# Three rearrangements of a four-layer kernel: the routing weights' transpose inside the pick, the last layer's loads inside its normalisation, and the third layer's indirect transfers divided differently over its stages

## The chip, the core and the metric

The kernel is one program on one core of one Trainium2 chip. The metric is the device time of one execution in microseconds. The core has five engines with a queue of instructions each: TensorE (PE), VectorE (DVE), ScalarE (ACT), GpSimd (POOL) and SyncE (SP, which here only issues transfers). GpSimd also issues the indirect transfers, the ones whose rows are chosen by an index tile.

## The reference

The input x is (8, 512, 128). Four layers follow, each of the form

```python
xn = layernorm(x)
s = attention_like(xn)      # another block in each layer
g = silu(ffn_like(xn))      # another mixture of experts or gated net in each
x = x + s * g
```

What matters here of the layers, which are numbered 0 to 3:

- Layer 1's attention keeps the outputs of only 153 of the queries of each head: a score for each query is made, and the highest 153 are picked. Its feed-forward net routes every token to 8 of 64 small experts, with weights that are normalised and scaled by 2.5.
- Layer 2's attention is a gated linear recurrence with a causal convolution of 4 taps ahead of it and unit-length keys and queries. Its feed-forward net is a mixture of 8 experts with 2 of them for each token and a capacity of 640 tokens for each expert, so tokens are packed by expert, computed, and fetched back.
- Layer 3 is softmax attention with 16 heads and a position bias, an output product and its bias `bo`, and a gated net whose weights are int32 and are scaled by 1/127.

## The kernel before, in words

Everything is resident in SBUF: `R.x` (the stream), `R.xnT` (the normalised stream, transposed), `R.s` and `R.f` (the two branches), each 128 partitions by 4096 floats. The work is a chain of phases. Each phase is one block: every engine gets its own list of instructions, waits go over semaphores, and at the end of the block all engines meet. When a phase with semaphores ends, one more short block clears them (`phase`, line 42 on). So phases never overlap; an engine that has nothing to do in a phase stands still until the slowest has finished. Eight groups of 512 tokens (B = 8, T = 512) are the usual loop inside a phase.

**Layer 1, between its attention and its output product.** `layer1_attention` runs the attention (`att1`), then `spread_phase` (line 1483), then `pick_phase` (line 1317), then the output product. `spread_phase` transposes the routing weights `comb` (32 tiles on PE, copied out of PSUM by ACT in 8 pieces) and has SP write them to DRAM as `cT` in 9 transfers, for which the block waits. VectorE meanwhile sets 4 rows of ones (`wt[NE:]`, line 1504) and clears `R.f` (line 1505). `pick_phase` is almost all VectorE: 20 rounds of `max` and `match_replace` over 128x512 scores, one after the other, with one transpose ahead of them and one behind. What it reads has nothing to do with `comb`.

**Layer 2.** `conv_phase` (16 steps c) makes queries, keys and values: PE does one product and a product of four taps a step, ACT and DVE the convolution of the values, DVE a transpose (line 2252), and POOL copies it to its place (line 2269). `unit_phase` scales queries and keys to unit length: ACT squares, PE sums, ACT and DVE take the inverse root, and then 16 products with `back` on PE (line 2318) are multiplied in by DVE (line 2330); PE may be four products ahead. Beside this work POOL issues 64 indirect scatters of 128 rows each (line 3207) that pack the tokens for the experts: two ahead of each of the 16 copies in `conv_phase`, and the other 32 one behind the other in `unit_phase`. `packed_experts_phase` waits for all of them. After `chunks_phase`, `recur_phase` runs the recurrence over 16 chunks as 8 bodies of 4 parts; POOL prepares `recur_st` for each part (line 2617) and issues an indirect gather of expert results (line 3231) behind three of the four parts, 24 in all. `output2_phase` gates and projects the result; in it POOL issues the other 40 gathers one behind the other. Its ACT and DVE combine the gathered rows in four parts (lines 2835 and 2883), each part once its own 16 gathers have landed.

**Layer 3.** `norm_phase` has an argument `ahead` for transfers that SP issues during it; for layer 3 it is empty. `layer3_attention` starts with SP issuing `bo` and eight pieces of `wo`, then the first weights, tokens and bias (lines 1827 to 1842). DVE copies `bo` into all of `R.s` (line 2043). `layer3_gate` starts with SP loading the int32 weights `wi` (line 1683), which DVE scales (line 1734) before PE can begin.

Of the kernel before, what the change touches and what calls it, by code (L numbers as in the profile page):

```python
# [8 lines left out]
P = 128  # L9
D = 128  # L10
B, T = 8, 512
NT = B * T // P
QT = T // P
# [1303 lines left out]
def pick_phase(nc, R, name, negmax, total, count, mask):  # L1317
# [3 lines left out]
    with phase(nc, name) as p:  # L1321
# [8 lines left out]
        s_sp, s_t, s_mk, s_m = p.sem("sp"), p.sem("t"), p.sem("mk"), p.sem("m")  # L1330
        scale = DH ** -0.5
        with nc.Block() as block:
            @block.vector
# [27 lines left out]
            def _(pe):  # L1361
# [3 lines left out]
                ins.then_inc(s_t, 1)  # L1365
                pe.wait_ge(s_mk, 1)
# [5 lines left out]
def layer1_attention(nc, R, t, early, out, sc, consts, s_in, comb, cT):  # L1372
    with ExitStack() as ctx:
# [12 lines left out]
        spread_phase(nc, R, "spread", comb, 64, cT)  # L1386
        pick_phase(nc, R, "pick", negmax, total, int(0.6 * 256), mask)
# [93 lines left out]


def spread_phase(nc, R, name, comb, NE, cT):

    ROWS = cT.shape[0]
    with phase(nc, name) as p:
        st = p.sb("st", [P, 2, QT, NE])
        wt = p.sb("wt", [ROWS, B * T])
        pt = p.ps("pt", [P, 2, T])
        s_one, s_st, s_t, s_wt, s_out = p.sem("one"), p.sem("st"), p.sem("t"), p.sem("wt"), p.sem("out")  # L1490
        NBODY = B // 2
        with nc.Block() as block:
            @block.sync
            def _(sp):
                sp.wait_ge(s_one, 1)
                sp.dma_start(cT[NE:, :], wt[NE:, :]).then_inc(s_out, 16)
                for n in range(B):
                    sp.wait_ge(s_wt, n + 1)
                    sp.dma_start(cT[:NE, n * T:(n + 1) * T], wt[:NE, n * T:(n + 1) * T]).then_inc(s_out, 16)
                sp.wait_ge(s_out, 16 * (B + 1))  # L1500

            @block.vector
            def _(dve):
                nc.vector.memset(wt[NE:, :], 1.0).then_inc(s_one, 1)
                nc.vector.memset(R.f[:, :, :], 0.0)

            @block.tensor
            def _(pe):
                for n in range(B):
                    if n >= 2:  # L1510
                        pe.wait_ge(s_wt, n - 1)
                    for q in range(QT):
                        ins = nc.tensor.transpose(pt[:NE, n % 2, q * P:(q + 1) * P], comb[:, n * QT + q], R.ident[:, :])
                    ins.then_inc(s_t, 1)

            @block.scalar
            def _(act):
                for n in range(B):
                    act.wait_ge(s_t, n + 1)
                    nc.scalar.activation(wt[:NE, n * T:(n + 1) * T], pt[:NE, n % 2], ACT.Copy).then_inc(s_wt, 1)  # L1520
# [145 lines left out]
def layer3_gate(nc, R, t):  # L1666

    U = 3
    with phase(nc, "glu") as p:
        wi = p.sb("wi", [P, 3, U, P], I32)  # L1670
# [6 lines left out]
        s_in, s_w, s_up, s_g, s_h, s_d, s_o, s_f = (p.sem(k) for k in ("in", "w", "up", "g", "h", "d", "o", "f"))  # L1677
        NBODY = B // 2
        IT = 2 * U
        with nc.Block() as block:  # L1680
            @block.sync
            def _(sp):
                sp.dma_start(wi[:, :, :, :].rearrange("p k u f -> p (k u f)"), t["w3"]).then_inc(s_in, 16)

# [77 lines left out]
def layer3_attention(nc, R, t):  # L1762
# [13 lines left out]
    with phase(nc, "att3") as p:  # L1776
        bias = p.sb("bias", [P, 2, 2 * BW])
        w = p.sb("w", [P, 2, 3, P])
        wo = p.sb("wo", [P, PAIRS, P])
# [11 lines left out]
        bo = p.sb("bo", [P, QT * D])  # L1791
# [4 lines left out]
        s_c = p.sem("c")  # L1796
# [27 lines left out]
        with nc.Block() as block:  # L1824
            @block.sync
            def _(sp):
                sp.dma_start(bo[:, :], t["bo3"]).then_inc(s_c, 16)
                for a in range(PAIRS):
                    sp.dma_start(wo[:, a], t["wo3"][a]).then_inc(s_c, 16)
# [1731 lines left out]
```

## Time and profile before

| | |
|---|---|
| median of 3 runs | 4108.3 us (4107.21 to 4111.95) |
| the profiled execution | 4112.44 us, of which 4110.6 us are the span from its first to its last instruction |
| PE busy | 3561.5 us (87%) |
| DVE busy | 2452.7 us (60%) |
| ACT busy | 2020.7 us (49%) |
| POOL busy | 1263.6 us (31%) |
| granted TensorE clock, mean | 0.911 of full speed |

The page's second part cuts the span into 40 slices of some 103 us; the busy tenths of PE, the granted clock and the DMA share are

```profile
PE   5799999959996788894999986788985599999997
PEclk9799999979997799996999987787687799999998
DMA  4322222100001311110666631030005233333330
```

The stages of this case lie where PE is low: slice 19 (spread and pick), slices 25 and 26 (convolution, unit length, experts), slices 30 and 31 (recurrence, output of layer 2, normalisation of layer 3), and the first and last slices of layer 3.

### The profile page before, as it was taken

The numbers are of one execution on the slowest core, as the hardware profiler recorded it, in microseconds if no ns is written. First come the engines' busy times: TensorE is split into PE (matmuls) and PEld (weight loads), VectorE is DVE, ScalarE is ACT, GpSimd is POOL, SyncE is SP. The second block draws the span as 40 slices with busy tenths as digits, with TensorE's granted clock in tenths as the row PEclk, the third lists the DMA queues.
The fourth block names the chain that finished last, engine by engine and source line by source line (L and its number), as shares of the span: only waits on it lengthen the run. The fifth ranks groups of instructions, "written<-read, shape, count | busy, mean of one in ns | idle before, by whom it ended". The sixth has DMA issues, their size and how long they took to land. (4 is left out here: it accounts for less than half of the span.)

```text
span 4110.6 us, 86910 instructions
## 1 busy us (share of the span) xinstructions
PE 3561.5 (87%) x28212; PEld 2164.2 (53%) x28212; DVE 2452.7 (60%) x5699; ACT 2020.7 (49%) x3970; POOL 1263.6 (31%) x1810
## 2 busy tenths in 40 slices
PE   5799999959996788894999986788985599999997
PEld 2344444437773222222677753268973366666664
DVE  5667677631113688885677776427645566666664
ACT  6466666633335477772333334233243465656562
POOL 0111111100001011110677762506474244444440
PEclk9799999979997799996999987787687799999998
DMA  4322222100001311110666631030005233333330
GB/s 128 79 55 57 54 58 54 48 11 6 11 6 49 76 46 43 42 30 13 176 163 157 157 83 61 34 101 3 3 17 72 80 116 114 117 113 117 114 104 27
DMA packets 198051, 287.18 MB, mean 70 GB/s; under 512 B 40922, under 2 KB 155296, under 8 KB 197460
## 3 DMA queue, kind: packets, MB, share of 16 engines
q1 hardware_dynamic: 193688, 275.28, 24.1%
q0 software_dynamic: 4096, 8.40, 1.5%
q8 instruction: 160, 2.62, 0.3%
q14 instruction: 107, 0.88, 0.1%
HBM read 232.38 MB, written 35.84 MB: 65 GB/s over the span
## 5 line engine op out<-in xcount | busy, mean ns | idle before, releaser
L709 ACT ACTIVATE att_E<-att_pX,att_gs 128x512 f32<-128x512 f32 (+3 forms) x1024 | 723.5, 740 | 423.5 <-PE att_pX L643 177.0
L742 DVE TENSOR_REDUCE att_mx<-att_pS 128x1 f32<-128x512 f32 (+4 forms) x960 | 732.4, 787 | 204.9 <-PE att_pS L617 173.0
L1855 POOL TENSOR_TENSOR att_E<-att_E,att_rz 128x128 f32<-128x128 f32 (+3 forms) x512 | 358.1, 720 | 435.3 <-DVE att_rz L2063 435.3
L637 PE MATMUL att_pX<-arr_qs,arr_ks 75*128 75x512 bf16 (+4 forms) x1536 | 427.3, 334 | 28.0 <-ACT att_E L709 12.8
L612 PE MATMUL att_pS<-arr_ks,arr_qs 72*128 72x512 bf16 (+4 forms) x1536 | 410.5, 339 | 44.1 <-DVE att_pO L732 12.6
L1583 POOL TENSOR_TENSOR pairs_h<-pairs_m,pairs_r 128x512 f32<-128x512 f32 x272 | 346.2, 1273 | 245.8 <-DVE pairs_m L1646 127.2
L574 POOL CAST att_mp<-att_m 16x128 bf16<-16x128 f32 x288 | 81.2, 282 | 935.2 <-DVE att_m L753 910.0
L1607 PEld LDWEIGHTS pairs_po<-pairs_a,pairs_h 128*128 128x128 f32 x2176 | 286.1, 192 | 130.2 <-issue 128.4
L654 PE MATMUL att_pO<-att_E,att_vs 128*9 128x512 f32 (+3 forms) x3072 | 328.9, 500 | 1.3 <-ACT att_E L709 1.3
L1628 ACT ACTIVATE pairs_r<-pairs_ph 128x512 f32<-128x512 f32 x272 | 162.6, 598 | 326.9 <-PE pairs_ph L1599 326.9
L1994 ACT ACTIVATE att_E<-att_S,att_nm 128x128 f32<-128x128 f32 (+3 forms) x512 | 282.0, 556 | 38.4 <-DVE att_nm L2057 38.4
L1599 PE MATMUL pairs_ph<-xnT,pairs_a 128*128 128x512 f32 x544 | 280.9, 599 | 10.2 <-DMA pairs_a<-in_down_dram 10.2
L637 PEld LDWEIGHTS att_pX<-arr_qs,arr_ks 79*128 79x128 bf16 (+1 forms) x1536 | 134.9, 98 | 294.1 <-ACT att_E L709 196.1
L1607 PE MATMUL pairs_po<-pairs_a,pairs_h 128*128 128x128 f32 x2176 | 287.5, 275 | 0.5 <-POOL pairs_h L1583 0.5
L1646 DVE SCALAR_TENSOR_TENSOR pairs_m<-pairs_ph,pairs_c 128x512 f32<-128x512 f32 x272 | 188.0, 692 | 140.0 <-ACT pairs_r L1628 132.8
L2057 DVE CUSTOM_DVE_ANT_0 att_S<-att_pS,att_bias 128x128 f32<-128x128 f32 (+3 forms) x512 | 230.5, 487 | 64.1 <-PE att_pS L1897 60.9
L612 PEld LDWEIGHTS att_pS<-arr_ks,arr_qs 76*128 76x128 bf16 (+1 forms) x1536 | 131.1, 99 | 240.3 <-DVE att_mx L742 149.1
L1252 PEld LDWEIGHTS ex_po<-ex_a,ex_h 128*128 128x128 f32 x1536 | 202.4, 192 | 92.0 <-issue 91.2
L1278 ACT ACTIVATE ex_h<-ex_ph,ex_bs 128x512 f32<-128x512 f32 x192 | 131.9, 687 | 214.5 <-PE ex_ph L1243 214.5
L1294 DVE SCALAR_TENSOR_TENSOR f<-ex_po,ex_ws,f 128x128 f32<-128x128 f32 x192 | 54.0, 344 | 277.4 <-PE ex_po L1252 277.4
L2071 DVE COPY att_WT<-att_pT 128x128 f32<-128x128 f32 (+2 forms) x384 | 179.2, 507 | 66.6 <-PE att_pT L1907 59.1
L1252 PE MATMUL ex_po<-ex_a,ex_h 128*128 128x128 f32 x1536 | 203.1, 275 | 0.0
(411 smaller groups left out, 6527.9 us busy)
## 6 DMA issues: line engine op xcount, KB each, us to landing
pairs_c<-weights SPq DMA_DIRECT2D x272, 256.0 KB, 3.9
att_bias<-in_bias_dram SPq DMA_DIRECT2D x64, 896.0 KB, 4.5
parts<-proj_part SPq DMA_DIRECT2D x144, 128.0 KB, 2.3
att_xb<-xnT SPq DMA_DIRECT2D x64, 256.0 KB, 2.7
arr_qs<-parts SPq DMA_DIRECT2D x192, 64.0 KB
arr_ks<-parts SPq DMA_DIRECT2D x192, 64.0 KB
att_w<-in_w3a_dram SPq DMA_DIRECT2D x64, 192.0 KB, 2.4
arr_qs<-parts SPq DMA_DIRECT2D x96, 96.0 KB
```

What stands on the lines that cost most here:

```text
L612: ins = nc.tensor.matmul(pS[:, bank, n * w:(n + 1) * w], qs[:K1, u, x, q * P:(q + 1) * P], ks[:K1, u, x, :w], start=(n == 0 or not causal) ...
L637: ins = nc.tensor.matmul(dst[:, n], ks[:, g % NB, x, kt * P:(kt + 1) * P], qs[:, g % NB, x, q0(kt):], start=(apart or n == 0), stop=not ca ...
L654: ins = nc.tensor.matmul(pO[32 * x:32 * x + DV, q0(kt):], vs[:, g % 2, x // maps, kt], E[:, kt % 2, x, :w], start=(kt == 0), stop=(kt == Q ...
L709: nc.scalar.activation(E[:, kt % 2, WIDE * xp:WIDE * (xp + 1), :w], places(c)[0], ACT.Exp, scale=gs[:, g % 2, gain_of:gain_of + 1]).then_i ...
L742: V.reduce_max(dst, src, AX.X).then_inc(s_mx, 1)
L1252: ins = nc.tensor.matmul(po[:, g % 2, q * P:(q + 1) * P], h[:, u % 2, q * P:(q + 1) * P], a2[:, v, u], start=(u == 0 and q == 0), stop=(u ...
L1583: nc.gpsimd.tensor_tensor(h[:, g % RING], m[:, g % RING], r[:, g % RING], ALU.mult).then_inc(s_h, 1)
L1599: nc.tensor.matmul(ph[:, g % RING], a[:, v, 0], R.xnT[:, b * T:(b + 1) * T], start=True, stop=True).then_inc(s_up, 1)
L1607: ins = nc.tensor.matmul(po[:, g % RING, q * P:(q + 1) * P], h[:, g % RING, q * P:(q + 1) * P], a[:, v, 1], start=True, stop=True)
L1855: nc.gpsimd.tensor_tensor(E[:, k, :width(j)], E[:, k, :width(j)], rz[:, u, k:k + 1].broadcast_to([P, width(j)]), ALU.mult).then_inc(s_n, 1)
L1994: nc.scalar.activation(E[:, k, :width(j)], S[:, r % RING, :width(j)], ACT.Exp, bias=nm[:, u, k:k + 1], scale=-1.0, accum_out=Z[:, u, k:k + ...
L2057: nc.vector.tensor_tensor_reduce(out=S[:, r % RING, :w_], in0=pS[:, r // 2 % 2, h, :w_], in1=bias[:, u, off:off + w_], scale=-1.0 / DW, sc ...
```

## The change

1. `spread_phase` is gone. Its work is inside `pick_phase`: PE does the 32 transposes of `comb` behind the first transpose of the scores, ACT copies them, SP writes them out, and the two memsets are on POOL in place of DVE. A phase with one semaphore is laid around the pick, so one more clearing block follows it.
2. In layer 3 `bo`, `wo` and `wi` have tiles in a new phase `pre3` around the whole layer, and SP loads them during `norm3`. The tiles and loads inside the two later phases are gone. One more clearing block ends the layer.
3. In `conv_phase` POOL issues three scatters ahead of each copy, in place of two; 16 are left for `unit_phase`. In `recur_phase` a gather follows every part, 32 in all; 32 are left for `output2_phase`.

```diff
 def pick_phase(nc, R, name, negmax, total, count, mask, comb, NE, cT, s_out):
+        wt = p.sb("wt", [cT.shape[0], B * T])
+        pW = p.ps("pW", [P, 2, T])
+            @block.gpsimd
+            def _(pool):
+                nc.gpsimd.memset(wt[NE:, :], 1.0).then_inc(s_one, 1)
+                pool.drain()
+                nc.gpsimd.memset(R.f[:, :, :], 0.0)
+            @block.sync
+            def _(sp):
+                for n in range(B):
+                    sp.wait_ge(s_wt, n + 1)
+                    sp.dma_start(cT[:NE, n * T:(n + 1) * T], wt[:NE, n * T:(n + 1) * T]).then_inc(s_out, 16)
+                sp.wait_ge(s_one, 1)
+                sp.dma_start(cT[NE:, :], wt[NE:, :]).then_inc(s_out, 16)
+                sp.wait_ge(s_out, 16 * (B + 1))
+            @block.scalar
+            def _(act):
+                for n in range(B):
+                    act.wait_ge(s_turn, n + 1)
+                    nc.scalar.activation(wt[:NE, n * T:(n + 1) * T], pW[:NE, n % 2], ACT.Copy).then_inc(s_wt, 1)
...
                 ins.then_inc(s_t, 1)
+                for n in range(B):
+                    if n >= 2:
+                        pe.wait_ge(s_wt, n - 1)
+                    for q in range(QT):
+                        ins = nc.tensor.transpose(pW[:NE, n % 2, q * P:(q + 1) * P], comb[:, n * QT + q], R.ident[:, :])
+                    ins.then_inc(s_turn, 1)
                 pe.wait_ge(s_mk, 1)
...
-        spread_phase(nc, R, "spread", comb, 64, cT)
-        pick_phase(nc, R, "pick", negmax, total, int(0.6 * 256), mask)
+        with phase(nc, "spread") as p:
+            pick_phase(nc, R, "pick", negmax, total, int(0.6 * 256), mask, comb, 64, cT, p.sem("out"))
...
# conv_phase
-                    aside(pool, c)
+                    for m in range(3 * c, 3 * c + 3):
+                        aside(pool, m)
# unit_phase
-                for n in range(N, 2 * N):
-                    aside(pool, n)
+                for m in range(3 * N, 4 * N):
+                    aside(pool, m)
# recur_phase
-                        if n < 3:
-                            gather(i * 3 + n)
+                        gather(i * IT + n)
# layer2_attention: scatter(pool, m) now issues one scatter a call, not two
-                output2_phase(..., gather, 3 * NC2 // 2, s_get)
+                output2_phase(..., gather, 2 * NC2, s_get)
...
 def layer3(nc, R, t, before):
-    norm_phase(nc, R, "norm3", before, lambda sp: None)
-    layer3_attention(nc, R, t)
-    layer3_gate(nc, R, t)
+    with phase(nc, "pre3") as p:
+        bo, wo = p.sb("bo", [P, QT * D]), p.sb("wo", [P, 8, P])
+        wi = p.sb("wi", [P, 3, 3, P], I32)
+        s_c, s_in = p.sem("c"), p.sem("in")
+        def ahead(sp):
+            sp.dma_start(bo[:, :], t["bo3"]).then_inc(s_c, 16)
+            for a in range(8):
+                sp.dma_start(wo[:, a], t["wo3"][a]).then_inc(s_c, 16)
+            sp.dma_start(wi[:, :, :, :].rearrange("p k u f -> p (k u f)"), t["w3"]).then_inc(s_in, 16)
+        norm_phase(nc, R, "norm3", before, ahead)
+        layer3_attention(nc, R, t, bo, wo, s_c)
+        layer3_gate(nc, R, wi, s_in)
```

## Rows read from the trace of the kernel before

**Rows 1.** Windows by stage: length, each engine's busy time (instructions), clock, DMA share, GB/s.

```profile
2547.00:2611.00 64.00, 59.04 (x138) 25.84 (x136) 47.91 (x71) 23.56 (x44) 46.41 (x46) 0.98 0.09 31
2637.00:2659.00 22.00, 10.31 (x10) 2.47 (x10) 4.26 (x7) 0.00 (x0) 13.52 (x15) 0.50 0.13 45
2659.00:2673.00 14.00, 12.31 (x14) 4.48 (x14) 7.35 (x11) 0.00 (x0) 0.00 (x0) 0.50 0.00 0
3105.00:3162.00 57.00, 19.99 (x66) 12.96 (x67) 23.05 (x30) 14.29 (x15) 39.26 (x40) 0.64 0.95 105
```

**Rows 2.** Timeline of DVE, spread and pick: start, length, engine, line, tiles, idle before.

```profile
1884.19 3.47 DVE L1504 MEMSET spread_wt<- 4x4096 f32 x1 [2.06 <-PEq L50]
...
1896.62 1.26 DVE L1337 SCALAR_TENSOR_TENSOR pick_sp<-total,negmax 128x128 f32<-128x128 f32 x4 [4.57 <-PEq L50]
...
1933.59 0.69 DVE L1358 COPY mask<-pick_pM 128x512 f32<-128x512 f32 x1 [1.21 <-PE pick_pM L1368]
1934.92 1.90 DVE L852 TENSOR_TENSOR out_hb<-heads,mask 128x512 f32<-128x512 f32 x3 [0.64 <-PEq L50]
```

**Rows 3.** Timeline of POOL, the widest memset it has in this kernel.

```profile
2763.72 0.53 POOL L2470 MEMSET chunks_a<- 128x512 f32 x1 [108.94 <-SPq L2379]
```

**Rows 4.** Timeline, start of layer 3's attention.

```profile
3229.90 0.33 SPq L1827 DMA_DIRECT2D att_bo<-in_bo_dram  x1
...
3234.08 0.43 SPq L1838 DMA_DIRECT2D att_w<-in_w3a_dram  x1
...
3238.01 2.05 PE L1882 MATMUL att_pA<-att_xb,att_w 128*128 128x512 f32 x2 [9.59 <-DVE s L2043]
```

**Rows 5.** Timeline, start of layer 3's gated net.

```profile
4024.20 1.28 ACT L1693 ACT_TABLE_LOAD   x1 [2.89 <-PEq L50]
4028.12 0.76 DVE L1734 TENSOR_SCALAR glu_w<-glu_wi 128x1152 f32<-128x1152 int32 x1 [4.81 <-DMA glu_wi<-in_w_dram]
```

**Rows 6.** Windows: layer 1's normalisation, with loads beside it, and layer 3's, without.

```profile
1267.40:1293.50 26.10, 6.70 (x24) 4.30 (x24) 22.43 (x96) 17.15 (x41) 11.03 (x8) 0.50 0.39 121
3198.70:3224.80 26.10, 6.69 (x24) 4.29 (x24) 22.45 (x96) 17.13 (x40) 11.07 (x8) 0.50 0.00 0
```

**Rows 7.** Timeline of POOL, one step of the convolution.

```profile
2551.27 0.61 POOL L2269 COPY x<-conv_vt 128x512 f32<-128x512 f32 x1 [0.68 <-DVE conv_vt L2252]
2552.04 1.20 POOL L3207 DMA_INDIRECT moe_in<-s,moe_put  x1 [0.16 <-issue]
2553.55 1.33 POOL L3207 DMA_INDIRECT moe_in<-s,moe_put  x1 [0.30 <-issue]
```

**Rows 8.** Timeline of DVE and POOL, second half of unit length.

```profile
2637.80 0.62 DVE L2330 TENSOR_TENSOR xnT<-unit_pB,xnT 128x512 f32<-128x512 f32 x1
...
2649.14 0.69 DVE L2330 TENSOR_TENSOR kb<-unit_pB,kb 128x512 f32<-128x512 f32 x1 [4.21 <-remote]
...
2653.82 0.96 POOL L3207 DMA_INDIRECT moe_in<-s,moe_put  x1 [0.30 <-issue]
...
2672.02 0.69 DVE L2330 TENSOR_TENSOR kb<-unit_pB,kb 128x512 f32<-128x512 f32 x1 [1.01 <-PE unit_pB L2318]
```

**Rows 9.** Timeline of DVE, the first instruction of three successive chunks of the recurrence.

```profile
3010.22 0.42 DVE L2726 SCALAR_TENSOR_TENSOR recur_Rr<-recur_pA,x 128x256 f32<-128x256 f32 x1 [2.05 <-PE recur_pA L2634]
...
3016.55 0.42 DVE L2726 SCALAR_TENSOR_TENSOR recur_Rr<-recur_pA,x 128x256 f32<-128x256 f32 x1 [2.33 <-PE recur_pA L2634]
...
3022.38 0.42 DVE L2726 SCALAR_TENSOR_TENSOR recur_Rr<-recur_pA,x 128x256 f32<-128x256 f32 x1 [1.93 <-PE recur_pA L2634]
```

**Rows 10.** Waits of POOL in the recurrence: for whom, us in total, times, longest.

```profile
POOL recur_st L2617 <- PE recur_pO L2667: 11.6, 13, 1.9
```

**Rows 11.** Timeline of ACT and POOL, layer 2's output.

```profile
3147.84 1.02 ACT L2825 ACTIVATE out_sg<-out_pg 128x1024 f32<-128x1024 f32 x1 [25.64 <-DMA arr_ks<-parts]
...
3155.78 0.95 POOL L3231 DMA_INDIRECT rows_r<-moe_out,moe_get  x1 [0.30 <-issue]
...
3161.99 1.02 ACT L2825 ACTIVATE out_sg<-out_pg 128x1024 f32<-128x1024 f32 x1 [13.12 <-DMA arr_ks<-parts]
```

More of the change, by code:

```diff
@@ L1313, in layer0_gate, with pick_phase @@
         experts_phase(nc, R, "ex0", 6, t["w1_0"], t["b1_0"], t["w2_0"], wts)
-def pick_phase(nc, R, name, negmax, total, count, mask):
+def pick_phase(nc, R, name, negmax, total, count, mask, comb, NE, cT, s_out):
     with phase(nc, name) as p:
@@ L1330, in pick_phase @@
         s_sp, s_t, s_mk, s_m = p.sem("sp"), p.sem("t"), p.sem("mk"), p.sem("m")
+        wt = p.sb("wt", [cT.shape[0], B * T])
+        pW = p.ps("pW", [P, 2, T])
+        s_one, s_turn, s_wt = p.sem("one"), p.sem("turn"), p.sem("wt")
         scale = DH ** -0.5
         with nc.Block() as block:
+            @block.gpsimd
[16 more added lines that the diff above has]
+                    nc.scalar.activation(wt[:NE, n * T:(n + 1) * T], pW[:NE, n % 2], ACT.Copy).then_inc(s_wt, 1)
             @block.vector
@@ L1480, in routing @@
         yield step
[L1483 to L1520, printed above, removed]
 def pairs_phase(nc, R, name, NPAIR, w1, w2, cT):
@@ L1676, in layer3_gate @@
         po = p.ps("po", [P, 2, T])
-        s_in, s_w, s_up, s_g, s_h, s_d, s_o, s_f = (p.sem(k) for k in ("in", "w", "up", "g", "h", "d", "o", "f"))
+        s_w, s_up, s_g, s_h, s_d, s_o, s_f = (p.sem(k) for k in ("w", "up", "g", "h", "d", "o", "f"))
         NBODY = B // 2
@@ L1680, in layer3_gate @@
         with nc.Block() as block:
-            @block.sync
-            def _(sp):
-                sp.dma_start(wi[:, :, :, :].rearrange("p k u f -> p (k u f)"), t["w3"]).then_inc(s_in, 16)
             @block.scalar
@@ L1758, in _, with layer3_attention @@
                 run_bodies(dve, NBODY, body)
-def layer3_attention(nc, R, t):
+def layer3_attention(nc, R, t, bo, wo, s_c):
     PAIRS, DW = 8, 64
@@ L1795, in layer3_attention @@
         pO = p.ps("pO", [P, T])
-        s_c = p.sem("c")
         s_z = p.sem("z")
@@ L1826, in _ @@
             def _(sp):
-                sp.dma_start(bo[:, :], t["bo3"]).then_inc(s_c, 16)
-                for a in range(PAIRS):
-                    sp.dma_start(wo[:, a], t["wo3"][a]).then_inc(s_c, 16)
                 def body(i, first, last):
@@ L3200, in layer2_attention, with scatter @@
         k, kd = kb[:, :], flat(R.s)
-        def scatter(pool, slot):
-            if slot == 0:
+        def scatter(pool, m):
+            if m == 0:
                 pool.wait_ge(moe.s_zero, 80)
-            for m in range(slot * 2, slot * 2 + 2):
-                n, j = divmod(m, 2)
-                nc.gpsimd.indirect_dma_start(moe.xin, bass.IndirectOffsetOnAxis(ap=moe.put[:, n, j:j + 1], axis=0), R.s[:, n], None).then_inc(moe.s_put, 16)
+            n, j = divmod(m, 2)
+            nc.gpsimd.indirect_dma_start(moe.xin, bass.IndirectOffsetOnAxis(ap=moe.put[:, n, j:j + 1], axis=0), R.s[:, n], None).then_inc(moe.s_put, 16)
         conv_phase(nc, R, "conv", (ws, ts, fold), q, k, v, scatter)
@@ L3233, in layer2_attention @@
                 recur_phase(nc, R, "recur", q, k, kd, inv, at_, last_g, v, own, s_c, gather)
-                output2_phase(nc, R, "out2", v, t["wg2"], t["nw2"], t["wo2"], park["s"], flat(R.s), k, moe, rows, park["x"], gather, 3 * NC2 // 2, s_get)
+                output2_phase(nc, R, "out2", v, t["wg2"], t["nw2"], t["wo2"], park["s"], flat(R.s), k, moe, rows, park["x"], gather, 2 * NC2, s_get)
 class Packed:
```

5 lines of the change are left out of this document (1 added, 4 removed).

## The prediction, made before the changed kernel was run

> **What bounds the kernel now.** No engine bounds the whole: every phase ends when its own slowest engine does. The page's chain of waits says little (it covers only the last instructions), so I went by the slices of the page for the places where PE is low, then by windows for each stage that the edits touch, then by the timeline inside each. The reader is to see four things.
>
> First, in the spread and the pick VectorE is the chain. It enters the spread at 1884.19, does nothing the pick needs, and enters the pick at 1896.62 [rows 2].
>
> Second, the convolution is bound by PE: busy 59.04 of 64 us at clock 0.98 [rows 1]. POOL follows: it waits 0.68 us of each step for the transpose that it copies [rows 7].
>
> Third, unit length and layer 2's output are bound by no engine while POOL issues indirect transfers back to back. In 2637 to 2659 PE is busy 10.31 of 22 us and DVE 4.26, yet each waits [rows 1]; DVE's multiplications, with up to four products ready, start 3 to 6 us apart, one after 4.21 us of a wait put down to "remote" [rows 8]. Once POOL's last scatter is issued at 2653.82 and has landed, PE runs without a gap: 12.31 of 14 us [rows 1]. In layer 2's output it is the same and worse: ACT stands 25.64 and 13.12 us before two activations whose products had been ready, and the second stand ends at 3161.99, 6 us after the last of 40 gathers is issued [rows 11]; over 57 us DVE is busy 23.05 and ACT 14.29, with the DMA engines at 0.95 [rows 1]. I read these stands as the work of the indirect transfers, since they end with them in both places. What exactly is held up (the fetching of instructions is my guess) the rows don't say.
>
> Fourth, layer 3's attention starts 8.1 us after SP's first issue (3229.90 to 3238.01) [rows 4], and its gated net 3.9 us after its block's start, on one load [rows 5].
>
> **Part 1, spread into pick.** VectorE can enter the pick when it entered the spread: 1896.62 - 1884.19 = 12.43 us go [rows 2]. The 32 transposes, 8 copies and 9 writes took until 1896 from 1883, some 13 us; started a microsecond or two later they end before 1900, while the 20 rounds run for 33 us more. PE's second need in the pick (the mask) comes after the rounds, so nothing waits behind the new transposes. Against it stands one more clearing block: pick's end (1933.59 + 0.69) to the next phase's first DVE instruction is 0.64 us for two block changes [rows 2], so 0.3. The memsets on POOL: 0.53 us for 512 elements a partition [rows 3] gives 8 x 0.53 = 4.2 for 4096, 8.5 for both; hidden under the rounds. If DVE stood still for all of them, 8.5 would come back: bounds -13 and -3.6. No row shows such a stand beside a POOL memset, so I take **-12.1**.
>
> [...]
>
> **Part 2, loads of layer 3.** SP issues ten loads during norm3. Layer 1's normalisation had its loads beside it, with the DMA engines at 0.39, and did exactly what layer 3's did without: 96 DVE instructions in 26.10 us each, busy 22.43 and 22.45 [rows 6]. So they cost nothing. In the attention the first weights were issued at 3234.08, behind nine loads that began at 3229.90 [rows 4]; now they go first, and all behind moves by 4.18 us. The trace names DVE's copy of `bo` as what PE waited for, but PE's wait is for weights and tokens; the copy ended at the same moment by chance, and with `bo` there it starts at the block's start. Bounds -5.8 (the copy alone) and -3. I take **-4.2**. In the gated net DVE no longer waits for the load: 4028.12 - 4024.20 = 3.92 [rows 5]; DVE may enter its block 0.3 later than ACT, and a clearing block adds 0.3: **-3.3**. Bounds -5 (PE stands 2.5 us and not 6.3 and might keep its clock: its first four products went at 1.2 GHz, some 0.42 us each too slow) and -2.5.
>
> **Part 3, scatters.** *Convolution.* A step of POOL is copy 0.61, gap 0.16, scatter 1.20, gap 0.30, scatter 1.33, then 0.68 of waiting: 4.28 in all, PE's own pace [rows 7]. A third scatter costs 0.30 + 0.96 when DVE leaves it alone [rows 8] and 0.30 + 1.33 when not [rows 7]. With 1.27 for it the step is 4.87 (all three undisturbed, 4.29; all disturbed, 5.23), POOL becomes what sets the pace, because DVE's transpose has two buffers and waits for POOL's copy. The last copy starts 15 steps behind the first, and the window of 64 us in rows 1 runs from the start of the first (2547.0) to the end of the last (2610.6): it would now end at 2547.0 + 15 x 4.87 + 0.6 = 2620.7: **+10.1**, bounds +1.3 and +15.5.
>
> *Unit length.* It issues 16 scatters, 1.266 us apart; 31 of these back from 2653.82 [rows 8] the first was at 2614.6, so now the last ends at 2634.9 on the old scale, and lands some 4 us later. DVE's first multiplication stays at 2637.80; from then PE runs its last 12 products at the spacing of the undisturbed end, 1.70 us each at half clock (1.01 idle + 0.69 busy on DVE [rows 8]; clock 0.50 [rows 1]): 2638.5 (the first multiplication's end) + 20.5 + 0.7 = 2659.7 and not 2672.7, **-13.0**. Bounds -23 (the clock is back at 2.4 GHz and DVE's 0.7 a step sets the pace) and 0 (the stands have another cause).
>
> *Recurrence.* The fourth gather sits behind the part where POOL waited; its waits were 11.6 us over 13 [rows 10], 0.9 each, a gather with its gap is 1.15, and POOL works half a body ahead, so POOL doesn't become the bound. But chunks with two gathers take longer than chunks with one: 6.33 against 5.83 here [rows 9], and over the 14 intervals of this instruction 6.60 (7 of them) against 5.99. Seven or eight chunks go from one to two: 7 x 0.6, **+4**, bounds 0 and +6.
>
> *Output.* Eight gathers fewer of 0.95 + 0.30 us [rows 11]: the last is issued 10.0 us earlier, and if the stands end with it, all that follows 3161.99 moves by as much: **-10.0**, bounds 0 and -14. The combining needs the last gathers only 20 us later.
>
> **Sum.** -12.1 - 4.2 - 3.3 + 10.1 - 13.0 + 4 - 10.0 = -28.5 us. The profiled execution took 4112.4, so 4083.9; it lies 4.1 above the median of the runs, whose time becomes 4108.3 - 28.5 = 4079.8, say **4080**.
>
> **The rivals.**
>
> *A. The stands are not the transfers' doing.* They then keep their length, and unit length and output gain nothing: -19.6 + 10.1 + 4 = -5.5, 4103. For it: in unit length the DMA engines were only 0.13 busy [rows 1], hardly enough to hold anything up. Against: both stretches of stands end within 4 to 6 us of the last issue. Chance 0.06.
> The Trainium skill speaks for this rival: "Runtime: NRT & Kernel Launch" (Instruction fetch mechanics) has each sequencer fetch blocks of 256 instructions over a queue of its own, "mostly hidden", and "DMA: Bandwidth & Descriptors" (SWDGE vs HWDGE vs iDMA) has each DMA engine go round its queues in turn. By that a fetch would not stand 25 us behind gathers.
>
> *B. The scatters turn cheaper than priced.* With DVE slower a step, the three scatters are undisturbed (+1.3 and not +10.1), and unit length gets its clock back (-23): -47, 4061. For it: 0.96 is the undisturbed length. Against: the clock stayed at 0.50 while PE was busy 12.31 of 14 us [rows 1]. Chance 0.10.
>
> *C. The convolution falls into the stands of unit length.* Scatters come every 2.14 us there now and every 1.27 in unit length; they will come every 1.6. If DVE and PE then meet a stand of some 3.6 us a step, as between the multiplications in unit length, 15 steps cost 54 more: 4134, slower. It decides the sign from 28.5 / 15 = 1.9 us a step on. Against it: at 2.14 there is hardly a stand, PE 0.92 busy. Chance 0.04.
>
> *D. The memsets hold DVE in the pick.* -3.6 there and not -12.1: 4088. Chance 0.08.
>
> **How the numbers follow.** The forecast has 0.72 and a range of its own of 4068 to 4092. Leaving out no more than 2 in 10, over B's side and toward A: 4064 to 4095. A difference of 0.2% (8 us) is about what can be told from none. Faster by more: forecast, B, D and a little of A, 0.90. Within: most of A and the dear end of part 3, 0.06. Slower: C, 0.04.
>
> **What would show it.** In the changed profile: the pick's first DVE instruction 2 us behind the end of att1 and its rounds at unchanged 1.60 us; POOL in the convolution without waits and its copies 4.9 us apart, with PE busy near 0.88; unit length ending some 25 us after POOL's last scatter, its multiplications 1.7 us apart from the second or third on; chunks of the recurrence all at 6.6; ACT's last stand in the output ending near 46 us after the block's start and not 57; PE in layer 3's attention 4 us after SP's first issue; DVE's scaling in the gated net at the block's start. The prediction is wrong if the copies in the convolution are further apart than 5.3 us, or if stands go on in unit length after the last scatter has landed.

## The result, and the profile after

| | before | after |
|---|---|---|
| median of 4 runs each | 4109.6 us (4107.2 to 4112.0) | 4079.4 us (4076.6 to 4083.9) |
| ratio | | 0.9924, 95% interval 0.9913 to 0.9936 |
| the profiled execution | 4112.4 us, span 4110.6 | 4083.9 us, span 4082.1 |

The forecast was 4080, and 4083.9 for the profiled execution. The median fell by 30.2 us and the profiled execution by 28.5; both are gains clear of the noise, as the interval stays below 1. Where the 28.5 us went, stage by stage, from the two timelines (unless its name says otherwise, a stage ends where the next one's first instruction stands):

| stage | before | after | difference | predicted |
|---|---|---|---|---|
| end of layer 1's heads to its output product (spread, pick) | 52.78 | 40.08 | -12.7 | -12.1 |
| convolution, first scatter to end of last copy | 75.52 | 83.44 | +7.9 | +10.1 |
| unit length, to the experts' first transfer | 62.82 | 50.38 | -12.4 | -13.0 |
| recurrence, to the output's first ACT instruction | 107.20 | 108.26 | +1.1 | +4 |
| layer 2's output, to layer 3's normalisation | 92.94 | 81.60 | -11.3 | -10.0 |
| layer 3's attention, SP's first issue to PE's first product | 8.11 | 3.25 | -4.9 | -4.2 |
| gated net, from ACT's table load to the final phase | 71.63 | 68.42 | -3.2 | -3.3 |
| all the rest | | | +7.0 | 0 |

The sum of the seven is -35.5; the rest of the program, unchanged, was 7.0 us longer in this execution (2.6 before the end of layer 1's heads, 2.8 between the pick and the convolution, 0.7 each in the experts with the chunks and in layer 3's attention, 0.2 in its normalisation). So some of the close agreement of the total is chance: single unchanged stages differ by 1 to 3 us from one execution to the next.

**The pick.** Timeline of the changed kernel (start, length, engine, line, tiles, idle before), the counterpart of [rows 2] and [rows 3]:

```profile
1884.45 0.29 DVE L766 TENSOR_TENSOR heads<-att_pMT,att_rz 128x128 f32<-128x128 f32 x1
...
1885.88 3.50 POOL L1338 MEMSET pick_wt<- 4x4096 f32 x1 [35.38 <-POOLq L50]
1885.93 1.27 DVE L1361 SCALAR_TENSOR_TENSOR pick_sp<-total,negmax 128x128 f32<-128x128 f32 x4 [1.19 <-PEq L50]
...
1889.00 0.69 DVE L1372 MAX8 pick_m<-pick_sT 128x8 f32<-128x512 f32 x1
...
1889.52 3.52 POOL L1340 MEMSET f<- 128x4096 f32 x1
...
1890.60 0.70 DVE L1372 MAX8 pick_m<-pick_sT 128x8 f32<-128x512 f32 x1
...
1924.82 1.90 DVE L852 TENSOR_TENSOR out_hb<-heads,mask 128x512 f32<-128x512 f32 x3 [1.02 <-PEq L50]
```

VectorE enters 1.2 us behind the heads, its rounds (MAX8 to MAX8) are 1.60 us apart beside POOL's second memset, and the extra clearing block shows as 1.02 us of idle time in place of 0.64. A memset of 4096 elements takes 3.5 us and not the 4.2 that I had scaled up from 512.

**Convolution.** Timeline of POOL, one step, against [rows 7]; then the groups of POOL in the window from first to last copy (busy, mean ns, idle before):

```profile
2564.46 1.25 POOL L3184 DMA_INDIRECT moe_in<-s,moe_put  x1 [0.17 <-issue]
2566.02 1.11 POOL L3184 DMA_INDIRECT moe_in<-s,moe_put  x1 [0.30 <-issue]
2567.43 1.34 POOL L3184 DMA_INDIRECT moe_in<-s,moe_put  x1 [0.30 <-issue]
2568.77 0.62 POOL L2248 COPY f<-conv_vt 128x512 f32<-128x512 f32 x1
...
2573.26 0.62 POOL L2248 COPY f<-conv_vt 128x512 f32<-128x512 f32 x1
```

```profile
L3184 POOL DMA_INDIRECT moe_in<-s,moe_put x45 | 49.8, 1107 | 11.6 <-issue 11.6
L2248 POOL COPY f<-conv_vt 128x512 f32<-128x512 f32 x8 | 5.2, 656 | 0.0
L2248 POOL COPY x<-conv_vt 128x512 f32<-128x512 f32 x8 | 5.0, 621 | 7.6 <-DVE conv_vt L2230 7.6
```

POOL is now what sets the pace: no wait ahead of its copies (the 7.6 us are the one ahead of the first). Windows of the changed kernel, columns as in [rows 1]: the convolution, unit length while its scatters run, its multiplications, the output up to ACT's last stand.

```profile
2539.50:2611.00 71.50, 59.03 (x138) 25.84 (x136) 51.80 (x71) 23.66 (x44) 59.84 (x61) 0.93 0.12 41
2616.70:2638.60 21.90, 19.99 (x40) 5.13 (x40) 6.57 (x2) 11.33 (x19) 15.39 (x16) 0.89 0.14 48
2638.60:2661.00 22.40, 20.84 (x24) 7.80 (x24) 10.75 (x17) 0.00 (x0) 0.00 (x0) 0.50 0.00 0
3095.00:3141.00 46.00, 19.44 (x65) 12.82 (x66) 23.35 (x30) 14.68 (x15) 31.75 (x32) 0.67 0.93 116
```

PE is busy 59.03 us in the convolution as before, now in 71.5 us and not in 64: a share of 0.83. The 0.88 that I had named was a slip, as 59 us in my own 73.7 is 0.80.

**Unit length.** Timeline of POOL and DVE, against [rows 8]: the last scatter is issued at 2635.74, and from the fifth multiplication on (2641.42) each starts 1.70 or 1.71 us after the one before.

```profile
2635.74 0.96 POOL L3184 DMA_INDIRECT moe_in<-s,moe_put  x1 [0.30 <-issue]
...
2638.64 0.62 DVE L2309 TENSOR_TENSOR xnT<-unit_pB,xnT 128x512 f32<-128x512 f32 x1
...
2641.42 0.69 DVE L2309 TENSOR_TENSOR xnT<-unit_pB,xnT 128x512 f32<-128x512 f32 x1 [0.37 <-PE unit_pB L2297]
2643.12 0.69 DVE L2309 TENSOR_TENSOR kb<-unit_pB,kb 128x512 f32<-128x512 f32 x1 [1.01 <-PE unit_pB L2297]
...
2660.19 0.69 DVE L2309 TENSOR_TENSOR kb<-unit_pB,kb 128x512 f32<-128x512 f32 x1 [1.01 <-PE unit_pB L2297]
```

**Layer 2's output and layer 3.** Timelines, against [rows 11], [rows 4] and [rows 5]:

```profile
3095.05 1.06 ACT L2797 ACTIVATE out_sq<-x 128x1024 f32<-128x1024 f32 x1 [2.44 <-DVE out_eps L2828]
...
3133.44 1.02 ACT L2803 ACTIVATE out_sg<-out_pg 128x1024 f32<-128x1024 f32 x1 [21.00 <-issue]
...
3135.50 1.23 POOL L3208 DMA_INDIRECT rows_r<-moe_out,moe_get  x1 [0.30 <-issue]
...
3140.60 1.02 ACT L2803 ACTIVATE out_sg<-out_pg 128x1024 f32<-128x1024 f32 x1 [6.14 <-remote]
...
3208.72 0.33 SPq L1816 DMA_DIRECT2D att_w<-in_w3a_dram  x1
3208.77 2.29 DVE L2021 COPY s<-pre_bo 128x4096 f32<-128x4096 f32 x1 [5.12 <-PEq L50]
...
3211.97 2.04 PE L1860 MATMUL att_pA<-att_xb,att_w 128*128 128x512 f32 x2 [4.67 <-DMA att_xb<-xnT]
...
3998.91 1.28 ACT L1678 ACT_TABLE_LOAD   x1 [2.86 <-PEq L50]
3998.94 0.76 DVE L1719 TENSOR_SCALAR glu_w<-pre_wi 128x1152 f32<-128x1152 int32 x1 [0.90 <-PEq L50]
```

ACT's last stand ends 45.6 us after the block's start (before: 56.9), 5.1 us after the last gather.

### The profile page after: what moved, and what is told of

Read it like the earlier page. It is cut to its first block and busy times, and to the rows that moved or that the text cites. A ratio compares the mean times of both kernels' runs of the same rounds, so it can differ in the third digit from the quotient of the medians.

```text
span 4082.1 us, 86911 instructions
## 1 busy us (share of the span) xinstructions
PE 3563.8 (87%) x28212; PEld 2170.8 (53%) x28212; DVE 2450.6 (60%) x5697; ACT 2022.2 (50%) x3970; POOL 1270.3 (31%) x1812
## 3 DMA queue, kind: packets, MB, share of 16 engines
q0 software_dynamic: 4096, 8.40, 1.4%
## 5 line engine op out<-in xcount | busy, mean ns | idle before, releaser
L1243 PE MATMUL ex_ph<-xnT,ex_a 128*128 128x512 f32 x384 | 198.3, 599 | 5.4 <-DMA ex_a<-in_w_dram 5.4
```

## The experiments

Twelve runs in four sessions (a session is a series of runs on one chip, the kernel before among them). In two of them (the first and the last) the kernel before took 4113.9 and 4112.4 us, near the 4109.6 of the comparison above. In the two between, which were on other chips and had one timed run a kernel, it took 4066.8 and 4071.3 us. That difference turned out to be the main finding. The stages of all kernels, defined as in the table above, in us. A "stand" is a time in which an engine waits although the work that it waits for has been done.

| kernel | pick | convolution | unit length | recurrence | output | layer 3 to PE |
|---|---|---|---|---|---|---|
| part 1 alone | 40.12 | 74.02 | 61.44 | 106.81 | 93.89 | 8.02 |
| part 2 alone | 52.84 | 75.46 | 62.25 | 107.39 | 93.61 | 3.41 |
| scatters alone | 52.87 | 83.49 | 50.78 | 107.24 | 93.25 | 8.19 |
| gathers alone | 52.82 | 74.11 | 61.23 | 108.80 | 82.70 | 8.11 |
| parts 1 and 2 (last session) | 40.25 | 74.06 | 62.37 | 106.20 | 92.62 | 3.22 |
| the changed kernel (last session) | 40.24 | 82.41 | 49.88 | 108.54 | 81.96 | 3.11 |
| transfers left out (4066.8) | 52.84 | 73.98 | 49.56 | 101.25 | 64.09 | 7.96 |
| memsets in their place (4066.8) | 52.86 | 75.18 | 48.48 | 100.12 | 64.00 | 8.17 |
| paced, no loads (4066.8) | 52.80 | 74.89 | 100.59 | 101.46 | 64.99 | 8.01 |
| paced, no loads (4071.3) | 52.80 | 75.47 | 100.63 | 102.23 | 64.60 | 8.07 |
| delayed and shifted (4066.8) | 40.16 | 82.35 | 49.86 | 104.36 | 63.98 | 3.10 |
| delayed and shifted (4071.3) | 39.81 | 83.63 | 50.53 | 104.59 | 64.91 | 3.12 |

### Each part by itself

Part 1 alone:

```diff
-        spread_phase(nc, R, "spread", comb, 64, cT)
-        pick_phase(nc, R, "pick", negmax, total, int(0.6 * 256), mask)
+        with phase(nc, "spread") as p:
+            pick_phase(nc, R, "pick", negmax, total, int(0.6 * 256), mask, comb, 64, cT, p.sem("out"))
```

> Part 1 alone on the kernel before: the spread inside the pick. By the prediction's sum the time falls by 12.1 us, to a ratio of 0.9971. If the whole gain of the change came from elsewhere, or one more clearing block and the memsets on POOL gave much back, it falls by less than 6 us. By the comparison of the two traces (52.78 us from att1's end to the output product before, 40.08 after) it should fall by 12.7.

Measured: ratio 0.9966 (0.9956 to 0.9977); of 4113.9 us that is a difference of -14.0 us (-18.1 to -9.5); the stage is 12.7 us shorter than in the three other kernels of the same session. Part 1 does what its step said.

Part 2 alone (the phase `pre3` and its ten loads):

```diff
-    norm_phase(nc, R, "norm3", before, lambda sp: None)
+        norm_phase(nc, R, "norm3", before, ahead)
```

> Part 2 alone: the ten loads of layer 3 during its normalisation. By the prediction -4.2 and -3.3, together -7.5 us, ratio 0.9982. A rival: the later start of PE was hidden behind the clock or behind the first tokens' load, then -3 to -4 us. The two traces say -4.9, -3.2 and +0.2 for the normalisation.

Measured: 0.9977 (0.9967 to 0.9986), -9.5 us (-13.6 to -5.8), and 3.41 us to PE's first product. The rival of a hidden start is outside the interval.

Scatters alone (3 a step, then 16):

```diff
-                    aside(pool, c)
+                    for m in range(3 * c, 3 * c + 3):
+                        aside(pool, m)
```

> Three scatters a step in the convolution and 16 in unit length, all else as before. By the prediction +10.1 - 13.0 = -2.9 us; by the traces +7.9 - 12.4 = -4.5 us, ratio 0.9989. If the stands in unit length had another cause than the scatters, the sum is +8 to +10 us, slower.

Measured: 1.0000 (0.9986 to 1.0013), -5.8 to +5.3 us. Its convolution and unit length together take 134.3 us; those of the three other kernels of the session 135.5, 137.7 and 135.3. So the shift of the scatters is worth 1 to 3 us there: what unit length gains the convolution pays. The interval takes in both the prediction's -2.9 us and the -4.5 us read from the two traces, so the time alone doesn't show that it gains anything. The case without any gain in unit length (+8 to +10) is excluded.

Gathers alone (one behind every part, 32 left for the output):

```diff
-                        if n < 3:
-                            gather(i * 3 + n)
+                        gather(i * IT + n)
```

> A gather behind each of the four parts of the recurrence and 32 in layer 2's output, all else as before. By the prediction +4 - 10.0 = -6.0 us; by the traces +1.1 - 11.3 = -10.2 us, ratio 0.9975. If the stands in the output were the work of its large loads and not of the gathers, about 0 to +1 us.

Measured: 0.9973 (0.9961 to 0.9984), -11.1 us (-16.0 to -6.6). The rival (stands that belong to the output's large loads, 0 to +1 us) is excluded, and the prediction's -6.0 lies just outside too. Recurrence +1.7 and output -10.9 against the mean of the three others. ACT's stand in the output, in the timelines of this kernel and then of the one with the scatters alone, which still has 40 gathers (the last one issued at 3139.27 and 3160.9):

```profile
3139.27 0.94 POOL L3230 DMA_INDIRECT rows_r<-moe_out,moe_get  x1 [0.30 <-issue]
...
3142.95 1.02 ACT L2824 ACTIVATE out_sg<-out_pg 128x1024 f32<-128x1024 f32 x1 [26.49 <-DMA arr_ks<-parts]
3145.25 1.02 ACT L2824 ACTIVATE out_sg<-out_pg 128x1024 f32<-128x1024 f32 x1 [1.27 <-DMA arr_ks<-parts]
```

```profile
3152.31 1.02 ACT L2826 ACTIVATE out_sg<-out_pg 128x1024 f32<-128x1024 f32 x1 [24.67 <-DMA arr_ks<-parts]
3167.16 1.02 ACT L2826 ACTIVATE out_sg<-out_pg 128x1024 f32<-128x1024 f32 x1 [13.83 <-DMA arr_ks<-parts]
```

The stands are cut up differently, but the last ends 6.0 and 6.3 us behind the issue of the last gather, 6.2 in [rows 11] and 5.1 in the changed kernel. In the other four profiles with stands it is 5.4 to 6.7 us, so the end of the stands goes with the transfers in every kernel that has stands.

### What makes the engines stand

The next four were to tell what in the transfers does it. Transfers left out, base the kernel before (the added block fills the tiles of gathered rows and costs 7.0 us):

```diff
-                for n in range(N, 2 * N):
-                    aside(pool, n)
...
-                for m in range(begun, 2 * NT):
-                    gather(m)
```

> Base is the kernel before. Left out: the 32 scatters of unit length and the 40 gathers of layer 2's output (a block that clears the gathered rows' tiles is added ahead of the recurrence). Theory T (the indirect transfers make the other engines stand): unit length takes 50.4 us from the last copy of the convolution to the experts' first transfer, as in the changed kernel and not 62.8, and in the output ACT's third gate product starts within 2 us of its product, so that the part up to ACT's last stand (57 us before) falls under 40 us. Rival L (the large loads of the output, or the stages' own handshakes): unit length stays at 62 us, and ACT stands on in the output while the loads run.

Memsets in the place of each of the 72 transfers:

```diff
+                for m in range(2 * N):
+                    nc.gpsimd.memset(fill[:, :], 0.0)
+                    pool.drain()
```

> As the run without those transfers, but in the place of each a POOL memset of 128x1408 of about 1 to 1.3 us, so that POOL is as busy as before and no transfer is issued. Theory T (transfers in flight): no stands, unit length 50.4 us. Rival P (a busy POOL holds VectorE and with it PE and ACT): unit length 60 us or more, multiplications 3 us apart and more while the memsets last.

Scatters paced by a memset, and the output's loads left out:

```diff
                 nc.gpsimd.indirect_dma_start(moe.xin, ..., R.s[:, n], None).then_inc(moe.s_put, 16)
+                if fill is not None:
+                    nc.gpsimd.memset(fill[:, :], 0.0)
...
-                    sp.dma_start(seq(xr, j), ...)
-                    sp.dma_start(R.x[:, n * SPAN:(n + 1) * SPAN, :], old[...])
```

> Base is the kernel before. Unit length: each of its 32 scatters is followed by a memset of about 0.9 us, so that they come some 2.3 us apart instead of 1.27. If the stands come from scatters issued faster than something drains, the multiplications end undisturbed (1.7 us apart, the last 49 us after the last copy of the convolution) although POOL goes on for some 75 us; if each scatter costs the others a fixed stand, they end at 62 us or later. Layer 2's output: the loads of the parked stream and of the parked normalised tokens are left out (4 MB), the 40 gathers stay. If gathers alone make the stands, ACT's last stand still ends near 57 us after the block's start; if the loads do it, or both together, it ends at 40 us or earlier.

Base the changed kernel, scatters delayed, ACT's instructions shifted:

```diff
+                pool.wait_ge(s_inv, 2)
                 for m in range(3 * N, 4 * N):
                     aside(pool, m)
...
+                for _n in range(48):
+                    act.nop(nofuse=True)
                 act.wait_ge(s_eps, 1)
```

> Base is the changed kernel. Unit length: its 16 scatters are held back until the second reciprocal has ended, so that they run beside the 16 multiplications. If stands need some 15 transfers of run-up, unit length stays at 50.4 us; if they belong to the kind of work (products and multiplications handing over to one another), it stands from the first of them on and takes 58 us or more. Layer 2's output: 48 empty instructions ahead of ACT's first. If the 21 us stand before ACT's third gate activation is the fetching of its instructions, it falls on another instruction or is gone; if it belongs to the gathers, it stays before the same one, 38 us after the block's start.

Measured, each in one run beside a kernel before of 4066.8 us: 4072.8, 4072.0, 4122.4 and 4051.4 us. All four showed no stand at all: output 64 to 65 us, multiplications undisturbed. (The paced kernel is slow because its 32 paced scatters take 100 us, for which the experts wait.) Read alone, each seems to prove its own theory, and they contradict one another: the loads had to be there for a stand, and were there in the last one; the gathers had to be there, and were there in the last two. What they share is the session. The kernel before was 41.5 us shorter in it than its 4108.3, and the stands that it has elsewhere are 62.82 - 49.56 = 13.3 and 92.94 - 64.09 = 28.8 us, together 42 (the recurrence adds some 6, and single unchanged stages differ by 1 to 3 us either way). And leaving 72 transfers out changed the time by +6.0 us, of which 7.0 are the added block: a gain of 1 us. A kernel before with stands would have become some 42 us shorter by it. So in that session the kernel before had none either. Two of the four were therefore run again:

> The same kernel as the run before it (base: the changed kernel; unit length's 16 scatters beside the multiplications; 48 empty instructions ahead of ACT's first in layer 2's output), once more, since the kernel before took 4066.8 us beside the last one and not 4108, 41.5 less: just the stands of unit length (12.4) and of the output (28.9) that all four of those runs lacked. If that chip has no stands whatever the kernel (theory C), then here, where the kernel before takes some 4110 us, unit length and output stand again: output 81 us and not 64, and the sum is near 4080. If the shift and the delay took the stands away, output stays at 64 us and the time is 4062 or less.

> The same kernel as the earlier run with paced scatters and without the output's large loads, once more. Where the kernel before takes some 4110 us: if stands come from scatters faster than something drains, the last multiplication ends 47 us after the convolution's last copy again; if each scatter holds the others, 58 us or more. Output: 65 us again if the loads are needed for the stands, 85 us or more if gathers alone make them.

Measured: 4057.8 and 4122.5 us beside 4071.3. The draw was again one without stands, so neither theory could be tried: stands that the kernel before doesn't have can't be taken away. What these six runs do give is the length of each stage without stands, and a fact on the load of the DMA engines. Windows of unit length and of the output: first of the kernel with transfers left out, then of the delayed one (clock and DMA share are the third and second number from the end):

```profile
2614.00:2660.00 46.00, 41.56 (x64) 13.01 (x64) 17.31 (x18) 11.93 (x19) 0.00 (x0) 0.69 0.00 0
3093.00:3157.00 64.00, 35.24 (x160) 23.62 (x160) 54.97 (x97) 28.83 (x51) 0.00 (x0) 0.81 0.22 71
```

```profile
2608.00:2652.50 44.50, 40.44 (x64) 12.85 (x64) 17.32 (x18) 11.93 (x19) 15.35 (x16) 0.69 0.07 24
3082.00:3146.00 64.00, 35.95 (x160) 24.38 (x160) 54.96 (x97) 28.83 (x51) 33.57 (x32) 0.80 0.72 103
```

With 32 gathers and 4 MB of loads in it, or with nothing, the output takes 64.0 us and its engines are busy for the same time. So neither POOL's work on a transfer nor a DMA share of 0.72 made an engine stand in that session.

The last session put the question to the two kernels with full transfers. The first leaves part 3 out:

```diff
-                    for m in range(3 * c, 3 * c + 3):
-                        aside(pool, m)
+                    aside(pool, c)
...
-                        gather(i * IT + n)
+                        if n < 3:
+                            gather(i * 3 + n)
```

> Parts 1 and 2 of the change; scatters and gathers divided as in the kernel before. Theory C (the stands come and go with the chip or the session, the kernel unchanged): beside a kernel before of about 4070 us, unit length takes 50 us and the output 64 us although all 32 scatters, 40 gathers and the output's loads are there; the gain is that of parts 1 and 2, some 22 us, 0.9946, and this kernel beats the changed one by 7 to 11 us. Rival K (the 48 empty instructions, the delayed scatters and the loads left out had taken the stands away in the runs before): unit length takes 62 us and the output 93. Beside a kernel before of about 4110 us both say 62 and 93, and the changed kernel is ahead by 7 us.

> The changed kernel itself, on the same chip as the version with parts 1 and 2 alone. Theory C, beside a kernel before of about 4070 us: -12.7 - 8.0 + 7.9 + 2.8 = -10 to -14 us, ratio 0.997, output 64 us. Rival K: -28.5 us, 0.993, output 81. Beside a kernel before of about 4110 us both say 0.993.

Measured, beside a kernel before of 4112.4 us: parts 1 and 2 alone 4093.6 us, 0.9955 (0.9940 to 0.9970), and the changed kernel 4080.0 us, 0.9924 (0.9911 to 0.9937). The stands were there again, on yet another chip, at the same places and of the same length. Timeline of DVE with parts 1 and 2 alone, unit length with 32 scatters (the last issued at 2646.8):

```profile
2637.96 0.69 DVE L2308 TENSOR_TENSOR xnT<-unit_pB,xnT 128x512 f32<-128x512 f32 x1 [2.81 <-PE unit_pB L2296]
2642.86 0.69 DVE L2308 TENSOR_TENSOR kb<-unit_pB,kb 128x512 f32<-128x512 f32 x1 [4.21 <-remote]
2647.76 0.69 DVE L2308 TENSOR_TENSOR xnT<-unit_pB,xnT 128x512 f32<-128x512 f32 x1 [4.21 <-issue]
```

So part 3 is worth 13.6 us between the medians there (12.5 by the stages: +8.4 - 12.5 + 2.3 - 10.7), and not the 7 us expected. In a session without stands it looks like a loss: there the same stages read +8.4 in the convolution (73.98 to 82.35), +0.3 in unit length, +3.1 in the recurrence, 0 in the output, about 12 us; and the delayed variant of the changed kernel gained 15.4 and 13.5 us on the kernel before (one run each), not 30. By the stages it should have gained 9 (-12.7 - 8.2 + 12), so the loss is 12 us by the stages and 5 to 7 by the times. Parts 1 and 2 alone would then be the better kernel there; that was not run. No kernel beat the changed one where stands occur.

**What is late.** The trace also records when each signal (semaphore increment) arrives, and that says more than the waits. The kernel before, layer 2's output, PE's third and fourth gate products, for which the two stands of [rows 11] wait:

```profile
3127.65 1.88 PE L2796 MATMUL out_pg<-xn2T,out_wgs 128*128 128x512 f32 x4
...
3131.16 1.88 PE L2796 MATMUL out_pg<-xn2T,out_wgs 128*128 128x512 f32 x4
```

They end at 3129.53 and 3133.04. Their signals are recorded at 3147.82 and 3161.96, and ACT starts at 3147.84 and 3161.99, as soon as it has them. In the delayed kernel, where there are no stands, ACT follows the third product at once:

```profile
3104.93 3.00 PE L2775 MATMUL out_pg<-xn2T,out_wgs 128*128 128x512 f32 x4
...
3107.97 1.03 ACT L2806 ACTIVATE out_sg<-out_pg 128x1024 f32<-128x1024 f32 x1 [8.68 <-PE out_pg L2775]
```

It is so throughout unit length, recurrence and output: in the runs without stands each signal of a PE product arrives 0.01 to 0.03 us behind its end, and in the others many come late there, in the kernel before by up to 15 us in unit length, 0.7 in the recurrence and 31 in the output. What waits for DVE or ACT in these stands starts within 0.05 us of their ends. In unit length of the kernel before, the signals of the products that ended at 2647.05, 2651.95 and 2657.61 came at 2659.62, 2659.66 and 2659.70, 4 us behind the last transfer's last packet. So most of a stand is PE's signal on its way. Not all of it: behind 3153 PE itself stands up to 2.4 us between products of one group, with nothing to wait for that the trace shows.

**What stays open:** why two sessions of four had no stands. Chip and session changed together (also the way of timing: one run there, many in the others); the kernel before was the same, and in those two it is known by its time alone. Open too is what holds PE's signals up. My guess in the prediction, the fetching of instructions, doesn't fit: ACT and DVE start 0.02 us behind the signal. The traffic says the same. Traffic of the kernel before by queue, in 2614 to 2620, then in 2640 to 2645, then in the output from 3106.5 to 3162 (packets, MB, share of 16 engines):

```profile
q0 software_dynamic: 104, 0.23, 11.1%
q14 instruction: 1, 0.01, 0.6%
...
q0 software_dynamic: 128, 0.26, 15.3%
...
q0 software_dynamic: 1236, 2.56, 77.9%
q1 hardware_dynamic: 1750, 3.29, 18.6%
```

From 2620 to 2660 no packet of an instruction queue appears, while DVE's multiplications stand and go on five times, and none in the output's two stands; and the transfers themselves flow at the same rate with and without stands, 25.6 packets a us here and in 2635 to 2645 of the delayed kernel. "Runtime: NRT & Kernel Launch" of the Trainium skill (Instruction fetch mechanics) has each engine's instructions come in blocks over a queue of its own; by that a stand ended by a fetch would show a packet at its end, and none does. The traces show two such queues for the five engines, so by itself this is no proof for each of them.

A backlog that builds up is a possible story: in unit length PE's signals are in time until 15.9 us behind the first issue in the kernel before and 17.8 in the changed one, and late from then on. In the changed kernel that is the end of its stretch of 16, and the four late signals (0.7 to 1.8 us) are hidden, since DVE is still at its second inverse; so the stretch shows no stand, but it isn't free of the effect. The paced kernel was to test that story, and ran where there was nothing to test. A rival that no run tests is the recording: where there are stands the trace has 619 to 787 of the 1024 arrivals that the 64 scatters signal, and where there are none it has them all, and every time here comes with a recorded span. Signals held up and records lost may have one cause, or the one may be the other's.

## Why the prediction was right, and where it was not

**Part 1** held to 0.6 us. The two memsets hid under the rounds, and rival D is out: the rounds stayed at 1.60. The four first instructions of the pick have two SBUF inputs each. "SBUF — State Buffer" in the Trainium skill (SBUF: two separate sides) has such a VectorE instruction contend only with a GpSimd instruction that reads SBUF, and a memset only writes. The trace agrees: they ran from 1885.93 in 1.27 us, 1.26 before [rows 2], beside the memset that had begun at 1885.88.

**Part 2** gave -4.9 and -3.2 us for -4.2 and -3.3. The normalisation cost +0.2 with its ten loads. PE began 3.25 us after SP's first issue; I had 4. Its wait is now for tokens (att_xb), as the prediction had said of weights and tokens, and not for DVE's copy.

**Convolution** was mis-sized by 2.2 us, with the mechanism right (POOL sets the pace, PE follows, no rival C). The term that failed is the 1.27 us for the third scatter: the 45 scatters average 1.107 us, the 30 before 1.221, so the step is 71.05 / 15 = 4.74 and not 4.87. Rival B had half its cause here: it said that scatters would be cheaper with DVE slower a step, and they were, though not down to 0.96. (The prediction's undisturbed step adds up to 4.25 and not 4.29.) The clock did not come back in the multiplications: 0.50, with PE busy 20.84 of 22.40 us.

**Unit length** was right in size (-12.4 for -13.0) and in its course: spacing 1.70 from the fifth multiplication on (I had said from the second or third), end 25 us behind the last scatter. That the first four came closer together, 0.5 to 0.6 us apart, is because their products had been made ahead. Rival A is out in every session in which it can be tested: A had +8 to +10 us for the scatters alone and about 0 for the gathers, measured were 0 (-5.8 to +5.3) and -11.1.

**Recurrence** is the step that failed most, +1.1 for +4 (+1.7 and +2.3 in the other sessions). I had read from 6.60 against 5.99 that a chunk with two gathers is dearer than one with one, and multiplied. Taken in turn the 14 intervals of the kernel before have means of 6.48 and 6.12, so the reading itself was too large: 7 x 0.36 = 2.5. Three successive chunks now, timeline of DVE as in [rows 9]:

```profile
3005.57 0.42 DVE L2704 SCALAR_TENSOR_TENSOR recur_Rr<-recur_pA,x 128x256 f32<-128x256 f32 x1 [2.28 <-PE recur_pA L2612]
3011.55 0.42 DVE L2704 SCALAR_TENSOR_TENSOR recur_Rr<-recur_pA,x 128x256 f32<-128x256 f32 x1 [2.25 <-PE recur_pA L2612]
3017.64 0.42 DVE L2704 SCALAR_TENSOR_TENSOR recur_Rr<-recur_pA,x 128x256 f32<-128x256 f32 x1 [2.28 <-PE recur_pA L2612]
```

The 14 intervals are 5.98 to 6.49 us with a mean of 6.31; before they were 5.59 to 7.23 with a mean of 6.30. Two gathers to every chunk did not give every chunk the price of the dear ones: part of that price was irregular. The table shows of which kind: with the same 24 gathers the recurrence takes 100 to 102 us in the sessions without stands and 106 to 107 in the others. It had stands in it which I had taken for the cost of the gathers: of PE's 128 signals 25 come over 0.1 us late in the kernel before, by up to 0.7 us and 12.1 us in all, 43 with 18.2 us in all in the changed one, and none where there are no stands. Where there are none, the eight more gathers cost 3 us, as POOL's own step of about 3 us a part becomes the pace.

**Output** was right in size, with 10.0 for 11.3 (10.9 and 10.7 in the other pairs): stands end 5 to 7 us behind the last gather. What the prediction did not see is how large the rest of the stand is: without stands the stage takes 64 us, and 18 of the 82 us after the change are still stand.

The total came out to within 1 us in part by luck: the stages that were moved gained 35.5 us and not 28.5, mostly by the recurrence and the convolution, and unchanged stages happened to take 7.0 us more.

## What to carry to other kernels

When engines stand beside a stretch of indirect transfers while their operands are ready, look where the stands end, and when the signals that the engines wait for arrive. If the stands end a nearly fixed time behind the last transfer, a transfer moved out of the stretch is worth about its issue time (eight gathers of 1.25 us gave 11.3 us in the output), until the stage's own work sets its end (16 scatters gave 12.4 us in unit length), and as long as the stage that takes it has a spare engine; once that engine sets the pace, as POOL did in the convolution, the price is nearly the same as the gain. Read a price "with against without" from a stage only if the stage is free of such stands. And run the base kernel beside every experiment on a wait: the four that seemed to remove the stands had only met a session without them, and only the time of the kernel before told.

## What the runs showed that was not expected

- The same kernel took 4108 to 4114 us in some sessions and 4067 to 4071 in others, at nearly the same mean clock (0.911 and 0.914), and the difference is about that of the stands in unit length, output and recurrence.
- Where engines stand, it is mostly PE's signals that arrive late: a product done at 3133.04 was signalled at 3161.96, and ACT started 0.03 us later.
- A busy DMA share is no sign of stands: 0.93 in the first 46 us of the output with them, 0.90 in the first 46 us of the delayed kernel's without.
- One POOL instruction `memset` of 128x4096 f32 takes 3.52 us and one of 4x4096 takes 3.50, and neither slowed VectorE beside it.
- Where they are unchanged, convolution and unit length still differ between profiles, 74.0 to 75.5 and (with stands) 61.2 to 62.8 us.
